# Keys mapped from PSUM, their product with x in three rounded parts, and statistics of x moved ahead

## What is computed

```
xn  = layernorm(x)
agg = segment_sum(xn[src], dst)                 # 20,000 edges
phi(t) = elu(t) + 1                             # = max(t + 1, exp(min(t, 0)))
q, k = phi(xn @ Wq + bq), phi(xn @ Wk + bk)     # 8 heads of 64
v    = xn @ Wv + bv
out  = (q @ (k^T v)) / (q . sum(k))             # per head
x    = x + gnn(xn, agg) + out @ Wp + bp
x    = x + experts(layernorm(x))
```

## Time and profile before

| what | value |
|---|---|
| median of 3 runs | 595.86 us (595.39 to 596.98) |
| time of the profiled execution | 595.98 us |
| its span in the profile | 594.2 us |
| busy: TensorE, VectorE, ScalarE, GpSimd | 86%, 61%, 42%, 15% |
| mean granted TensorE clock | 0.96 |

### The profile page before, as it was taken

One profiled execution on the slowest core, in us unless ns is written; L12 is line 12 of the kernel. 1 busy time (PEld: TensorE's weight loads), 2 busy tenths in 40 slices (PEclk: granted clock), 3 DMA queues, 4 the chain that ended last, 5 costly groups with the idle time before them and its releaser, 6 DMA issues.

```text
span 594.2 us, 8244 instructions
## 1 busy us (share of the span) xinstructions
PE 510.9 (86%) x2685; PEld 352.9 (59%) x2685; DVE 365.4 (61%) x1030; ACT 247.8 (42%) x498; POOL 88.8 (15%) x93
## 2 busy tenths in 40 slices
PE   1679999999989999999999999944999999877800
PEld 0334444454579888899999998822454555444400
DVE  4887778767865565378882324973665665644236
ACT  2899777688535442066662223431222222212100
POOL 4001101100000000000000000034344454431210
PEclk9999999999989999999999999967999999999965
DMA  9500000000100019500052006979899999999758
GB/s 308 171 1 2 1 1 1 1 1 2 43 29 0 1 28 381 221 1 2 0 225 95 0 1 258 419 285 411 286 412 416 416 412 416 414 412 406 266 205 341
DMA packets 29432, 108.25 MB, mean 182 GB/s; under 512 B 5019, under 2 KB 6044, under 8 KB 21580
## 3 DMA queue, kind: packets, MB, share of 16 engines
q1 hardware_dynamic: 19148, 88.18, 37.7%
q0 software_dynamic: 5120, 10.26, 4.5%
q10 hardware_dynamic: 5120, 9.26, 4.4%
HBM read 95.58 MB, written 18.63 MB: 192 GB/s over the span
## 4 chain that ended last, share of the span: by engine, by line
PE 73%; DMA 10%; SPq 5%; DVE 4%; issue 4%; ACT 3%; DVEq 0%; POOL 0%; POOLq 0%
PE PS L495 8%; PE PS L494 8%; PE PS L496 8%; PE PS L768 8%; PE PS L783 7%; PE PS L569 6%; PE PS L532 5%; DMA BIG<-in_we 5%; PE PS L524 4%; PE PS L598 4%; PE PS L599 4%; SPq L1468 4%; PE PS L710 3%; PE PS L558 2%; DMA BIG<-y_rows 2%
## 5 line engine op out<-in xcount | busy, mean ns | idle before, releaser
L494 PE MATMUL PS<-ROUND 128*128 128x416 f32 (+3 forms) x232 | 83.7, 361 | 0.0
L495 PE MATMUL PS<-ROUND 128*128 128x416 f32 (+3 forms) x232 | 83.5, 360 | 0.0
L496 PE MATMUL PS<-ROUND 128*128 128x416 f32 (+3 forms) x232 | 83.4, 359 | 0.0
L783 PE MATMUL PS<-BIG 128*64 128x512 f32 x232 | 55.0, 593 | 1.4 <-issue 0.8
L997 DVE BATCH_NORM_STATS2 BST<-BIG 128x6 f32<-128x416 f32 (+1 forms) x36 | 20.7, 590 | 43.8 <-ACT BIG L1334 35.2
L598 PE MATMUL PS<-ROUND 128*128 128x416 f32 (+3 forms) x120 | 44.5, 371 | 2.3 <-DVE ROUND L914 1.8
L494 PEld LDWEIGHTS PS<-ROUND 128*128 128x128 f32 (+1 forms) x232 | 43.5, 188 | 2.6
L496 PEld LDWEIGHTS PS<-ROUND 128*128 128x128 f32 (+1 forms) x232 | 43.6, 188 | 2.5
L898 DVE TENSOR_TENSOR BIG<-PS,BIG 128x280 f32 (+17 forms) x69 | 30.8, 446 | 23.0 <-PE PS L558 18.2
L495 PEld LDWEIGHTS PS<-ROUND 128*128 128x128 f32 (+1 forms) x232 | 43.5, 188 | 2.4
L1181 DVE COPY BIG<-PS 128x512 f32<-128x512 f32 x24 | 16.6, 692 | 45.8 <-PE PS L783 45.8
(11 more groups left out here) (237 smaller groups left out, 904.3 us busy)
## 6 DMA issues: line engine op xcount, KB each, us to landing
BIG<-in_we SPq DMA_DIRECT2D x54, 1024.0 KB
XA<-in_we SPq DMA_DIRECT2D x6, 1024.0 KB
y_rows<-KVB SPq DMA_DIRECT2D x19, 256.0 KB
BIG<-y_rows SPq DMA_DIRECT2D x9, 512.0 KB, 6.6
BIG<-in_we SPq DMA_DIRECT2D x8, 512.0 KB, 13.2
BIG<-in_wqkvp ACTq DMA_DIRECT2D x3, 1024.0 KB, 14.6
XA<-in_x SPq DMA_DIRECT2D x9, 256.0 KB, 10.1
xx_rows<-XA ACTq DMA_DIRECT2D x9, 256.0 KB
```

Source lines behind the costliest of these rows:

```text
L494: mm(o, ah, bh, start=first, stop=False)
L495: mm(o, ah, bl, start=False, stop=False)
L496: return mm(o, al, bh, start=False, stop=last)
L783: ins = mm(PS[64 * j:64 * j + 64, b, :], HT[:, s, 128 * f2 + 64 * j:128 * f2 + 64 * j + 64], buf[:, 1024 + 512 * f2:1024 + 512 * f2 + 512] ...
```

## The change

The batches of the statistics become two, tiles 0 to 1 and tiles 2 to 9, and all ten `st` are moved to the head of VectorE's list. `xh` and `xl` of a tile are moved from after the mapping, and from the first chunk of `agg`, to the time of its `kmm`. The bias of K is split into two fp32r rows (`bkh`, `bkl`) and added by two fp32r products with a row of ones behind the four of `kmm`. `kadd` is gone. `kexp` reads PSUM, and `phi` reads PSUM and the Exp and frees the bank. `gmm` becomes three fp32r products for each of its four (high by high, high by low, low by high) and needs two new steps a tile: `ph` (ScalarE, rounding of the mapped keys) and `pl` (VectorE, the rest). In the queries the Identity is gone, and `qphi` reads PSUM with the bias and frees the bank. `pair` becomes 5.5.

```diff
-BATCH = [(0, 1), (1, 3), (3, 6), (6, 10)]
+BATCH = [(0, 2), (2, NT)]
...
-    begin, pair, unit, turn = 12.0, 6.0, 2.7, 1.5
+    begin, pair, unit, turn = 12.0, 5.5, 2.7, 1.5
...
-    at(11.2, "prep", 0)
+    at(9.2, "prep", 0)
...
+    at(13.6, "bkh")
+    at(13.7, "bkl")
     for i in range(NT):
-        at(8.3 + 1.7 * i, "st", i)
-    for q, (a, b) in enumerate(BATCH):
-        at(8.3 + 1.7 * (b - 1) + 0.5, "sq", q)
-        at(8.3 + 1.7 * (b - 1) + 0.9, "rr", q)
+        at(8.3 + 0.3 * i, "st", i)
+    for q, t in enumerate((8.8, 13.0)):
+        at(t, "sq", q)
+        at(t + 0.4, "rr", q)
...
+        at(k + 0.3, "xh", i)
+        at(k + 1.1, "xl", i)
         for q in range(4):
             at(k + pair * q / 8, "kmm", i, q)
-            at(k + pair * (1.45 + q / 8), "gmm", i, q)
-        at(k + pair / 2 + 0.3, "kadd", i)
-        at(k + pair / 2 + 1.2, "kexp", i)
-        at(k + pair / 2 + 2.4, "phi", i)
-        at(k + pair / 2 + 3.2, "xh", i)
-    done = begin + pair * (NT + 0.95)
+            at(k + pair * (1.6 + q / 8), "gmm", i, q)
+        at(k + pair / 2 + 0.3, "kexp", i)
+        at(k + pair / 2 + 1.5, "phi", i)
+        at(k + pair / 2 + 2.1, "ph", i)
+        at(k + pair / 2 + 2.9, "pl", i)
+    done = begin + pair * (NT + 1.1)
...
-            if c == 0:
-                at(base + turn * i - 1.7, "xl", i)
...
-                    ins = mm(PS[0:n, b, :], XT[:, k, cs], WK[:, k, :], start=(k == 0), stop=(k == 3))
+                    ins = mm(PS[0:n, b, :], XT[:, k, cs], WK[:, k, :], start=(k == 0), stop=False)
                     if k == 3:
-                        ins.then_inc(full[b], 1)
+                        if i == 0:
+                            pe.wait_ge(s_bkl, 1)
+                        mm(PS[0:n, b, :], ONER[:, 0:n], BKH, start=False, stop=False)
+                        mm(PS[0:n, b, :], ONER[:, 0:n], BKL, start=False, stop=True).then_inc(full[b], 1)
...
-                        pe.wait_ge(s_phi, i + 1)
-                    ins = mm(PS[:, 4 + k, :], XN[0:n, i, 128 * k:128 * k + 128], PHI[i % 4][0:n, :], start=(i == 0),
-                             stop=(i == NT - 1))
+                        pe.wait_ge(s_pl, i + 1)
+                        pe.wait_ge(s_xl, i + 1)
+                    f = slice(128 * k, 128 * k + 128)
+                    ins = products(PS[:, 4 + k, :], XNH[0:n, i, f], XNL[0:n, i, f], PHIH[i % 4][0:n, :], PHIL[i % 4][0:n, :],
+                                   i == 0, i == NT - 1)
...
-                    if c == 0:
-                        pe.wait_ge(s_xl, i + 1)
...
+                    dve.wait_ge(s_ke, i + 1)
+                    V.scalar_tensor_tensor(PHI[i % 4][0:n, :], PS[0:n, b, :], 1.0, TMP[0:n, 2 * (i % 2) + 1, :], ALU.add,
+                                           ALU.max).then_inc(moved[b], 1)
+                elif kind == "pl":
+                    i, n = step[1], rows(step[1])
+                    dve.wait_ge(s_ph, i + 1)
...
+                    V.tensor_tensor(PHIL[i % 4][0:n, :], PHI[i % 4][0:n, :], PHIH[i % 4].bitcast(F32)[0:n, :],
+                                    ALU.subtract).then_inc(s_pl, 1)
...
                     dve.wait_ge(s_qe, 4 * c + r + 1)
-                    V.tensor_tensor(QT[:, r, o:o + w], QT[:, r, o:o + w], TMP[:, 2 * (r % 2) + 1, 0:w],
-                                    ALU.max).then_inc(s_q, 1)
+                    V.scalar_tensor_tensor(QT[:, r, o:o + w], PS[:, b, 0:w], BQ1[:, r:r + 1], TMP[:, 2 * (r % 2) + 1, 0:w],
+                                           ALU.add, ALU.max).then_inc(moved[b], 1)
...
-                    A.activation(QT[:, r, o:o + w], PS[:, b, 0:w], ACT.Identity, bias=BQ1[:, r:r + 1]).then_inc(moved[b], 1)
```

More of the change, by code:

```diff
@@ L334, in gnn_mix_moe @@
         PHI = [TMP[:, 0, :], TMP[:, 2, :], big(KK0, 512), big(KK0 + 512, 512)]
+        PHIL, PHIH = ([rounded(QT0 + 2048 * a + 512 * q, 512) for q in range(4)] for a in range(2))
+        BKL, BKH, ONER = (rounded(a, w)[0:1, :] for a, w in ((BR0, 512), (BR0 + 512, 512), (QT0 + 4096, 128)))
         BK, BP = big(BR0, 512), KSB[:, :, :].rearrange("p r e -> p (r e)")
@@ L576, in tensor @@
                     pe.wait_ge(moved[bk], uk)
-                    pe.wait_ge(s_q, 4 * c + 4)
+                    for r in (2, 3):
+                        bq2, uq2 = at_of(("q", r, c))
+                        pe.wait_ge(moved[bq2], uq2)
                     b, use = bank(step)
@@ L847, in vector @@
                     V.tensor_scalar(RP1[:, q], RR[:, q], 1.0, None, ALU.add).then_inc(s_rr, 1)
[L848 removed]
+                elif kind == "bkl":
+                    dve.wait_ge(s_bkh, 2)
+                    V.tensor_tensor(BKL, BK[0:1, :], BKH.bitcast(F32), ALU.subtract).then_inc(s_bkl, 1)
+                elif kind == "phi":
                     i = step[1]
                     n, (b, use) = rows(i), at_of(("k", i))
[L851 to L852 removed]
                     if i >= 4:
                         dve.wait_ge(s_ksum, i - 3)
[L855 to L863 removed]
+                    dve.wait_ge(s_ke, i + 1)
[4 more added lines that the diff above has]
+                    dve.wait_ge(s_ph, i + 1)
+                    if i >= 4:
+                        dve.wait_ge(s_g, i - 3)
+                    V.tensor_tensor(PHIL[i % 4][0:n, :], PHI[i % 4][0:n, :], PHIH[i % 4].bitcast(F32)[0:n, :],
+                                    ALU.subtract).then_inc(s_pl, 1)
                 elif kind == "ksc":
@@ L902, in vector @@
                     o, w = CH[c]
+                    b, use = at_of(("q", r, c))
+                    if r == 0 and c == 0:
+                        dve.wait_ge(s_ope, 3)
+                        for bg, ug in plan["gts"]:
+                            dve.wait_ge(full[bg], ug)
                     dve.wait_ge(s_qe, 4 * c + r + 1)
-                    V.tensor_tensor(QT[:, r, o:o + w], QT[:, r, o:o + w], TMP[:, 2 * (r % 2) + 1, 0:w],
-                                    ALU.max).then_inc(s_q, 1)
+                    V.scalar_tensor_tensor(QT[:, r, o:o + w], PS[:, b, 0:w], BQ1[:, r:r + 1], TMP[:, 2 * (r % 2) + 1, 0:w],
+                                           ALU.add, ALU.max).then_inc(moved[b], 1)
                 elif kind == "xl":
@@ L1248, in scalar @@
                                  scale=-1.0).then_inc(s_soa, 1)
+                elif kind == "bkh":
+                    act.wait_ge(sd_brow, 48)
+                    A.copy(BKH, BK[0:1, :]).then_inc(s_bkh, 1)
+                    act.wait_ge(s_pool, 4)
+                    A.copy(ONER, KVB[0:1, 0, :]).then_inc(s_bkh, 1)
                 elif kind == "kexp":
                     i, n, (b, use) = step[1], rows(step[1]), at_of(("k", step[1]))
-                    u, w = PHI[i % 4][0:n, :], TMP[0:n, 2 * (i % 2) + 1, :]
-                    act.wait_ge(moved[b], use)
+                    w = TMP[0:n, 2 * (i % 2) + 1, :]
                     if i >= 2:
-                        act.wait_ge(s_phi, i - 1)
-                    A.activation(w, u, ACT.Relu, bias=ONE[0:n, :], scale=-1.0).then_inc(s_kr, 1)
+                        bo, uo = at_of(("k", i - 2))
+                        act.wait_ge(moved[bo], uo)
+                    act.wait_ge(full[b], use)
+                    A.activation(w, PS[0:n, b, :], ACT.Relu, scale=-1.0).then_inc(s_kr, 1)
                     act.wait_ge(s_kr, i + 1)
                     A.activation(w, w, ACT.Exp, scale=-1.0).then_inc(s_ke, 1)
+                elif kind == "ph":
+                    i, n, (b, use) = step[1], rows(step[1]), at_of(("k", step[1]))
+                    act.wait_ge(moved[b], use)
+                    if i >= 4:
+                        act.wait_ge(s_g, i - 3)
+                    A.copy(PHIH[i % 4][0:n, :], PHI[i % 4][0:n, :]).then_inc(s_ph, 1)
                 elif kind == "gts":
@@ L1391, in gpsimd @@
                 if kind == "phi":
-                    i, n = step[1], rows(step[1])
+                    i, n, (b, use) = step[1], rows(step[1]), at_of(("k", step[1]))
                     u = PHI[i % 4][0:n, :]
-                    pool.wait_ge(s_phi, i + 1)
+                    pool.wait_ge(moved[b], use)
                     if i == 0:
```

32 lines of the change are left out of this document (11 added, 21 removed).

## The result

The median after is 600.21 us (8 runs, 598.30 to 601.80) against 596.50 us (8 runs, 594.41 to 598.26) for the kernel before in the same rounds. The ratio is 1.006, with a 95% interval of 1.0036 to 1.0083: slower, by about 3.7 us. The forecast was 2.2 us faster. The profiled executions have spans of 600.0 and 594.2 us.

A forecast was written before the change was run, and what follows sets the result against it. TensorE was taken to bound the keys by its work, with the start waiting for ScalarE and VectorE. Terms -2.4, +0.3, +2.8, +0.8 and -3.7 sum to -2.2 us: 593.7 us from 595.86, range 590 to 599 us.

The forecast's parts named there:

- Part 2: Keys, bias on TensorE: two fp32r products at 0.233 us each, +0.47 us a tile, +3.3 us for tiles 3 to 9.
- Part 5: Queries: `qphi` frees the bank instead of ScalarE, and `z` 0 and `zr` move; +0.8 us, between 0 and +3.
- Part 6: First chunk of `agg`: the wait for `xl` and the slow products behind it go; -3.7 us, lower bound -1.8.
- Part 1: Keys, `gmm` as three fp32r products: 0.70 us instead of 0.86, -5.7 us from tile 1 on.
- Part 3: Keys: VectorE and ScalarE get about 56 us of work each, under TensorE; +0.3 us for collisions of in-order queues.
- Part 4: Start: statistics first delay the first products, four table loads go from ScalarE; +2.8 us, bounds 0 and +5.3.
- the start costs no more than it saves: Rival for the start: ScalarE alone sets that stage, +2.8 us falls to 0, time 591 us; chance 0.15.
- The rival with VectorE as the bound: Rival for the keys: added VectorE work, caught by GpSimd's KSUM, makes VectorE the bound, 599 us; chance 0.22.

The follow-up runs named there:

- one_bias: Kernel after with one bias product of 64 rows in place of two of one row; 597.94 us, 1.0024 of the kernel before.
- bias_128: Kernel after with one bias product of 128 rows behind `kmm` in place of two of one row; 595.66 us, 0.9979 of the kernel before.
- bias_first: Kernel after with the two bias products of tiles 1 to 9 ahead of `kmm` instead of behind it; 599.78 us, 1.0058 of the kernel before.
- stats_before: Kernel after with the statistics in four batches and `st` and `prep` at their old places; 598.12 us, 1.0033 of the kernel before.
- no_bias: Kernel after with the two bias products left out, so the keys have no bias; 591.23 us, 0.9908 of the kernel before.
- best_128: Kernel after with `z` 1 in bank 3 and one bias product of 128 rows, ahead of `kmm` from tile 1; 591.92 us, 0.9907 of before.
- z_bank3: Kernel after with `z` 1, the second divisor product, in bank 3 instead of bank 5; 596.77 us, 0.9992 of the kernel before.
- kadd_back: Kernel after with the bias of K added by VectorE again, no bias products, and bank 3 for `z` 1; 592.28 us, 0.9924 of before.
- xl_early: Kernel before with `xl` moved behind `gmm`, out of the first chunk of `agg`; 595.61 us, 0.998 of the kernel before.
- gmm_fp32: Kernel after with `gmm` as one fp32 product again in place of three fp32r; 607.04 us, 1.0186 of the kernel before.

## Why the prediction was wrong, point by point

The forecast put the start of the second chunk at 178.82 - 2.2 = 176.6 us. It came at 181.46. (The text beside it names 158 and 175.5 us for `agg`, which is 1.1 us earlier than its own sum gives, 159.2 and 176.6. I compare with the sum.) The miss is 4.8 us there, and 5.9 in the medians. The 1.1 us between is not located. It lies within what the rest of the kernel varies by. Two steps of the forecast failed: the price of the bias products (part 2), and the claim that nothing else holds the first chunk of `agg` (parts 5 and 6).

**Part 1, three parts: right.** 0.62 us a tile measured, 0.64 forecast.

**Part 2, the bias: the term was mis-sized.** "I take 0.233, because the columns that stream are the same", and nothing to 0.233 as bounds. It is 0.75 to 0.8 us a tile instead of 0.47. For tiles 3 to 9 that is 2.1 us more. The upper bound was taken from products with 128 rows among others with 128 rows. The columns do cost 0.23 us a product (one_bias against the pair), and on top comes 0.34 us a tile for going from 128 rows to few and back. It comes once, for two products of one row and for one of 64, and not at all for one of 128 (bias_128). Nor is it the format (bias_128, bias_first). The timelines show that the weights of the first narrow product are loaded no earlier than it begins, and those of the second, and of the product with 128 rows in best_128, ahead. That late loads at the two changes are the whole of the 0.34 us is argued from these rows, not shown. One row and 64 rows were never tried in the same number of products.

**Part 3, VectorE in the keys: right.** No wait over 0.5 us between 46 and 105 us. VectorE is busy 53.13 and ScalarE 52.77 us there, less than the 56 of the forecast. `phi` from PSUM takes 0.689 us and the old `phi` took 0.688, so the 60 and 125 ns of the Trainium skill (Perfetto Trace Analysis, Optimizing Scalar/DVE Operations) don't show here. `qphi` from PSUM is another matter: 0.63 us for 416 columns where 0.586 was taken before, 0.05 us each, and hidden. (Its operation changed too, to one with a bias, so the 0.05 isn't shown to be PSUM's.) I charged 0.3 us for collisions, and there was less waiting than before: 0.51 us where 1.11 us was waited, by 109 us.

**Part 4, the start: its size was right, its reason only in part.** `kmm` 2 was to end at 45.4 us. Its last bias product starts at 44.81 us, and an edge group follows at 45.13. Of TensorE's timeline after, the wait for `bkl` and the start of the second tile:

```profile
18.56 5.40 PE L529 MATMUL PS<-BIG 128*128 128x512 f32 x6 [0.68 <-ACT BIG L1240]
...
26.14 0.49 PE L533 MATMUL PS<-ROUND 1*128 1x512 f32 x1 [0.94 <-DVE ROUND L860]
...
30.32 3.75 PE L529 MATMUL PS<-BIG 128*128 128x512 f32 x4 [1.36 <-DVE BIG L867]
```

The forecast blamed the order of the statistics for +2.8 us, with the bias pairs of the first three tiles in it (part 2 charges tiles 3 to 9). By the same reckoning it is 2.6 us (45.13 - 41.75, + 0.25 - 1.06), but stats_before gets only 0.5 to 1.7 us of it back. Three to four bias pairs lie in this stage too, and no_bias reaches tile 4 2.0 us earlier than the kernel after. They look like the larger part, though starts of the same list lie up to 1.3 us apart. So the agreement in size is partly luck. The rival *the start costs no more than it saves* was nearer the truth about the order, and was no gain, because its 591 us stood on the other terms.

**Part 5, the queries: the wait was put at the wrong place.** From ks to `agg` it takes 1.06 us more, about 0.7 of it edge groups that had been in the keys: 0.4 instead of 0.8. I saw `z` 0 move in the list, and counted its reciprocal as a burden on VectorE only. I didn't ask which bank `z` 1 fills and who needs it next.

**Part 6, `xl` out of `agg`: right, and hidden by that.** "Nothing else holds them: (...) `zr` is not on their way" was said of the last tiles of the chunk, where it is true. At the first tile `zr` is on the way: 4.1 us more than the 17.4 us forecast, 2.2 of them the wait and most of the rest the low clock behind it. z_bank3 gives 3.8 us of it back by a bank number alone. The 3.7 us that part 6 takes off are themselves a wait and a low clock: the slow products of the earlier trace rows ran at a granted clock of 0.57 (174 to 178 us, before).

The sum of the misses at the second chunk: +2.1 for the bias, -0.2 in the start, -0.3 for collisions that did not come, -0.6 for the smaller wait by 109 us, -0.4 in the queries and +4.1 in `agg` make 4.7 of 4.8 us. With both causes undone the gain is there: best_128 has the second chunk at 174.09 us, 2.5 us ahead of the forecast's 176.6, and 591.92 us. Its one product of 128 rows costs 0.23 us a tile less than the two of the forecast, 1.6 us over seven tiles.

**The rival with VectorE as the bound** gave 599 us, near to the result, by a mechanism that was not there (no_bias, kadd_back). Its price is real, though. `pl` takes 0.69 us alone and 1.22 us when it meets the KSUM sum (timeline after, VectorE and GpSimd):

```profile
67.36 0.69 DVE L874 TENSOR_TENSOR ROUND<-BIG,ROUND 128x512 fp32r<-128x512 f32 x1 [0.88 <-ACT ROUND L1283]
...
74.08 1.28 POOL L1425 TENSOR_TENSOR KSUM<-KSUM,BIG 128x512 f32<-128x512 f32 x1 [8.22 <-DVE BIG L867]
74.69 1.22 DVE L874 TENSOR_TENSOR ROUND<-BIG,ROUND 128x512 fp32r<-128x512 f32 x1 [0.40 <-ACT ROUND L1283]
```

That fits the Trainium skill (SBUF — State Buffer, Who interferes with whom): the later of the two blocks. In the kernel after `pl` was caught twice in ten tiles (757 ns in the mean of seven between 46 and 112 us). In xl_early `xl` was caught four times in eight, and TensorE lost nothing by it.

## What to carry to other kernels

When a change moves a step against its neighbours, follow the buffer that the step holds as well as the engine that it runs on: a reciprocal on an engine with time to spare cost 2.2 us of waiting through one PSUM bank, 3.8 to 5.0 us where a low clock followed (after, bias_128), and another bank number repaired it. Look for due times that are fixed or clamped when a period in the plan is shortened, since the steps hung on them fall behind the others. A product added to an engine that sets the pace has to be priced by a row of its own shape, rows of the contraction included, and among neighbours like its own. Moving work to that engine from one with time to spare gains little: the bias cost the same on either engine at best (kadd_back, best_128), and 0.6 us a tile more in the form chosen.

## What the runs showed of the hardware

- An fp32r product of 512 columns takes 0.23 us among products of 128 rows. Two of one row between products of 128 rows take 0.80 us together (after against no_bias), one of 64 rows 0.58 us (one_bias), one of 128 rows 0.23 us (bias_128): 0.23 us each, and 0.34 us once for changing to few rows and back. The 98-row products of `agg` are 0.19 us apart like those of 128 rows beside them (180.13 to 181.46 us in the kernel after), so it isn't any number under 128.
- After a wait of 2.16 us for one reciprocal the granted clock was 0.59 between 163 and 167 us, and the products that followed lost another 1.3 us. The same wait was followed by a clock of 1.00 in no_bias and gmm_fp32. Waits of 1.78 us (before, at 174.15 us) and 1.68 us (xl_early, at 109.47 us) were followed by 0.57 and 0.63. Waits of 0.46 us (z_bank3) and 1.21 us (kadd_back) were followed by no such stretch.
- A subtraction on VectorE of two 128x512 f32 operands takes 0.68 us, and 1.20 to 1.57 us when it starts inside a GpSimd addition of 1.3 us (one `pl` in the kernel after, four `xl` in xl_early).
